# Five expert tiles from an early table, the rest of the table beside them, and scatters held until the step's denominators are summed

## The chip, the cores and the metric

The kernel runs on one core of one Trainium2 chip. The metric is device time in microseconds for one launch, taken on that core. TensorE is called PE, VectorE DVE, ScalarE ACT, GpSimd POOL and SyncE SP, as the profile does.

## The reference, cut to what matters

64 images are cut into 169 patches each (10,816 tokens of 128 features). The tokens go through a linear attention block and then through eight experts, of which each token takes its best two.

```python
concat = jnp.concatenate((x, lu, ru, ld, rd), axis=1)            # five shifted copies of each image
normed = (concat - mean) * rsqrt(var + EPS) * gamma + beta
h = conv(normed, W, stride 8).reshape(B, D, 169).transpose(0, 2, 1)     # B=64, D=128

q, k, v = split(layernorm(h) @ Wqkv.T)                           # 8 heads of 64
q_prime = exp((q * scale) @ proj.T);  k_prime = exp(k @ proj.T)
D_inv   = 1.0 / (einsum("bhnf,bhf->bhn", q_prime, k_prime.sum(axis=2)) + 1e-6)
context = einsum("bhmf,bhmd->bhfd", k_prime, v)
h = h + (einsum("bhnf,bhfd->bhnd", q_prime, context) * D_inv[..., None]) @ Wout.T + bout

topv, topi = top_k(layernorm(h) @ Wg, 2);  w = softmax(topv)
for e in range(8):                                               # y starts at zero
    y += gw[..., e] * ((silu(x @ W[e]) * (x @ V[e])) @ W2[e])    # x = layernorm(h), F = 512
h = h + y
```

## The kernel before, in words

**Token stage.** Images are taken two at a time: 32 pairs (NPAIR), in groups of four steps (k = 0 to 3) for which one patch preparation is made ahead. `step(n, k, ...)` is written once for each engine and unrolled over n = 0 to 34. In step n four pairs are in work at once: pair n is convolved and normalised (flag `a`), pair n-1 gets its keys, queries and context (`b`), pair n-2 its attention output (`c`), pair n-3 its routing to experts (`d`). Steps 32 to 34 are the drain: `a` is off, then `b`, then `c`. Each engine runs its own list in order; semaphores tie the lists.

**Inside a step, PE** does q features 0 and 1 of pair n-1, the softmax denominators of pair n-2 (line 578, 32 small products into bank 7, counted by `d8_done`), the convolution of pair n (line 585), q feature 2, then the broadcast of the inverted denominators (line 529), for which it needs DVE's chain: `dsum` (line 874, waits for `d8_done`), reciprocal (876), rounding (888, 894). Keys, the attention output (647), the context (698, 704), the residual with the gate's logits (667) and the folded output weights (711) follow. Two products (552, 553) add up how many earlier tokens chose each expert: the `ranks`, kept in bank 2, which the residual product also uses.

**DVE** finds the two best experts (`best`, `choose`) and in `place` turns ranks into row numbers (`sloti`, line 1020). The running counts per expert are in `counts`.

**POOL** takes two roots a step for the layer norms (lines 1225, 1227) and scatters: for each pair six indirect DMAs (line 1245) write 128 rows each to `sorted_rows` in DRAM, sorted by expert. In step n it issues the rows of pair n-4: three before the first layer norm's root and three after it, when `sloti` and the weights are there and `d8_done` shows the denominators of the **previous** step. In step 31 and in the drain it scatters pair n-3 as well, three, then two scatters before the second root.

**Between the stages.** After step 34 DVE makes the table of the 92 expert tiles of 256 rows (lines 1034 to 1061; row number, expert, and how many output DMAs to wait for), all on one partition. SP and ACT write pad rows behind each expert's last row (line 354). PE runs idle products (543: 2, 3 and 8 of them; 717: 39) meanwhile. Then SP waits for the table, the pads and all scatters, and loads the first tile's rows (line 1330).

**Expert stage.** Per tile PE turns the rows (two products, line 1344), makes both hidden products (24, line 1356) and the output (16, line 1368); ACT copies the expert's weights (1391) and takes the silu (1407); DVE splits weights and rows into two parts (1422, 1433), multiplies (1440) and scales the output by the gate (1446, 1448); POOL adds two times 128 rows to the output in DRAM (line 1483). A tile's scaling waits for the landing of the additions two tiles before, since they share a buffer. Additions of a tile also wait for those of the tile before, unless both belong to one expert. The unused tiles of the 92 are the first ones; they read and write pad rows.

## Time and profile before

| | us |
|---|---|
| median of 3 runs | 1214.05 (1208.42, 1214.05, 1215.71) |
| the profiled execution's own time | 1208.1 |
| its span in the trace | 1206.3 |
| granted PE clock, mean share of full speed | 0.976 |
| busy: PE, DVE, ACT, POOL | 1119.9, 878.5, 561.3, 627.1 |
| first turn of rows of the expert stage | 742.12 from the start |

The profile page gives each engine's busy time over the whole span, then the chain of work that ended last, then the costliest groups of instructions with the idle time that stood in front of them and what ended it. A busy share is a mean over two stages that have different limits, so the steps of the token stage are best read one at a time. A released wait named "remote" is one whose end the profile cannot tie to an instruction that ended just then. Ends of PE's instructions are modelled; the events of its semaphores are recorded.

### The profile page before, as it was taken

How to read it: one execution, taken by the hardware profiler on the slowest of the kernel's cores; microseconds unless marked ns; L12 is line 12 of the kernel's file. 1: busy time of each engine (PE TensorE's matmuls, PEld its weight loads, DVE VectorE, ACT ScalarE, POOL GpSimd, SP SyncE). 2: the span in 40 equal slices, each digit the busy share in tenths (PEclk: the TensorE clock that was granted, in tenths of full speed). 3: DMA queues.
4: the chain of work that ended last, by engine and by line, in shares of the span. 5: the costliest groups of instructions: out<-in, count | busy, mean ns of one | idle time of the engine just before them, and what ended most of it. 6: DMA issues, size and time to landing. Idle time of an engine off the chain costs nothing.

```text
span 1206.3 us, 30227 instructions
## 1 busy us (share of the span) xinstructions
PE 1119.9 (93%) x8672; PEld 949.0 (79%) x8673; DVE 878.5 (73%) x3310; ACT 561.3 (47%) x1307; POOL 627.1 (52%) x656
## 2 busy tenths in 40 slices
PE   4899999899899899999998779999999999999996
PEld 4577667667677676676666558999999999999995
DVE  6477777777687777776875656777777777777774
ACT  3534435436345354354333213555555555555552
POOL 0014435344444344354443544677777777777675
PEclk9899999999999899999999989999999999999999
DMA  8160201210301202110010313344344444444442
GB/s 179 39 178 26 76 24 35 71 31 29 75 31 37 62 29 68 35 33 27 28 31 22 89 49 84 48 59 54 51 54 53 58 53 55 53 54 55 56 55 29
DMA packets 76010, 65.58 MB, mean 54 GB/s; under 512 B 12339, under 2 KB 66803, under 8 KB 75927
## 3 DMA queue, kind: packets, MB, share of 16 engines
q0 software_dynamic: 32704, 24.99, 14.8%
q1 hardware_dynamic: 41990, 38.71, 12.9%
q10 hardware_dynamic: 1232, 0.85, 0.3%
q8 instruction: 42, 0.69, 0.2%
q14 instruction: 42, 0.34, 0.1%
HBM read 32.81 MB, written 31.71 MB: 53 GB/s over the span
## 4 chain that ended last, share of the span: by engine, by line
PE 67%; DVE 16%; issue 5%; another core or an unknown queue 4%; DMA 2%; POOL 2%; ACT 1%; SPq 1%; POOLq 0%; DVEq 0%; ACTq 0%
PE bank L1356 20%; PE bank L1368 13%; PE bank L647 5%; PE bank L698 4%; DVE patches L798 3%; PE bank L685 3%; PE bank L711 3%; PE bank L687 3%; PE bank L686 3%; PE bank L704 2%; DVE rparts L888 2%; PE bank L447 2%; PE bank L585 2%; DVE rden L876 2%
## 5 line engine op out<-in xcount | busy, mean ns | idle before, releaser
L1483 POOL DMA_INDIRECT out_rows<-yo,dest x184 | 327.6, 1780 | 135.6 <-issue 89.4
L1356 PE MATMUL bank<-xT_e,wv 128*128 128x256 f32 x2208 | 287.0, 285 | 0.9 <-DVE xT_e L1433 0.9
L1356 PEld LDWEIGHTS bank<-xT_e,wv 128*128 128x128 f32 x2208 | 270.1, 189 | 1.2 <-DVE xT_e L1433 1.2
L1245 POOL DMA_INDIRECT sorted_rows<-xrow_all,sloti x192 | 190.0, 990 | 62.3 <-issue 52.3
L1407 ACT ACTIVATE sil<-bank 128x256 f32<-128x256 f32 x368 | 141.1, 384 | 160.8 <-PE bank L1356 141.4
L1368 PE MATMUL bank<-w,hid 128*128 x1472 | 179.7, 275 | 2.7 <-DVE hid L1440 2.7
L1368 PEld LDWEIGHTS bank<-w,hid 128*128 128x128 f32 x1472 | 171.5, 192 | 3.2 <-issue 3.2
L1440 DVE TENSOR_TENSOR hid<-sil,bank 128x256 f32<-128x256 f32 x368 | 145.0, 417 | 25.1 <-ACT sil L1407 22.2
L1422 DVE TENSOR_TENSOR wv<-wv_all,wv 128x1024 fp32r<-128x1024 f32 x92 | 112.7, 1225 | 67.7 <-issue 36.3
L1160 ACT ACTIVATE attn<-bank 128x256 f32<-128x256 f32 x128 | 49.3, 386 | 196.2 <-PE bank L687 164.8
L1391 ACT CAST wv<-wv_all 128x1024 fp32r x92 | 96.2, 1046 | 39.0 <-issue 39.0
L1265 POOL COPY xrow_all<-xrow_all 128x384 f32<-128x384 f32 x32 | 16.1, 503 | 178.1 <-issue 159.7
L585 PE MATMUL bank<-patches,wct 128*128 128x338 f32 x320 | 101.0, 463 | 0.0
L1225 POOL TENSOR_SCALAR vare<-mv 128x3 f32<-128x3 f32 x64 | 12.4, 193 | 165.4 <-issue 117.4
L798 DVE TENSOR_TENSOR patches<-bank,gam 128x416 f32<-128x416 f32 (+3 forms) x160 | 71.6, 502 | 26.3 <-PE bank L447 25.6
L711 PE MATMUL bank<-wvo,attn 128*64 128x136 f32 x1024 | 76.4, 288 | 6.2 <-ACT attn L1155 4.0
L585 PEld LDWEIGHTS bank<-patches,wct 128*128 128x128 f32 x320 | 59.3, 193 | 28.7 <-issue 1.1
L647 PE MATMUL bank<-attn 128*128 128x169 f32 x512 | 79.5, 307 | 0.6 <-DVE attn L855 0.6
L529 PE MATMUL bank<-rparts,pick_head 104*128 104x340 f32 x128 | 47.5, 372 | 33.7 <-DVE rparts L894 32.0
L1175 ACT ACTIVATE attn<-bank 128x512 f32<-128x512 f32 x96 | 57.4, 598 | 44.8 <-PE bank L687 39.0
L647 PEld LDWEIGHTS bank<-attn 128*128 128x128 f32 x512 | 73.9, 189 | 1.7 <-DVE attn L855 0.8
L1155 ACT COPY attn<-bank 128x272 f32<-128x272 f32 x128 | 49.8, 390 | 48.4 <-PE bank L711 41.8
(191 smaller groups left out, 1936.2 us busy)
## 6 DMA issues: line engine op xcount, KB each, us to landing
xr<-sorted_rows SPq DMA_DIRECT2D x92, 130.0 KB
raw<-in_x SPq DMA_DIRECT2D x64, 84.5 KB
raw<-in_x SPq DMA_DIRECT2D x60, 78.0 KB
out_rows<-attn SPq DMA_DIRECT2D x64, 58.5 KB
sorted_rows<-xrow_all,sloti POOLq DMA_INDIRECT x192
out_rows<-yo,dest POOLq DMA_INDIRECT x184
wv_all<-in_L_ffn_W SPq DMA_DIRECT2D x8, 256.0 KB, 5.6
wv_all<-in_L_ffn_V SPq DMA_DIRECT2D x8, 256.0 KB, 5.7
```

Source lines behind the costliest of these rows:

```text
L585: t = pe.matmul(bank[1][:, 0:PT], wct[:, q], patches[:, par, q, 2 * k:2 * k + 2].rearrange("p b t -> p (b t)"), start=(q == 0), stop=(q == 4))
L647: t = pe.matmul(bank[7][:, TOK * i:TOK * i + TOK], mm[:, pc, i, j, 0:D], qf[:, pc, j, TOK * i:TOK * i + TOK], start=(j == 0), stop=(j == 3))
L711: t = pe.matmul(o_[64 * (h % 2):64 * (h % 2) + 64, col:col + D + HEADS], gT[:, i, NF * h:NF * h + NF], wvo[:, h], start=True, stop=True)
L798: t = ve.tensor_tensor(dst[:, lo:hi], src[:, i0:i0 + hi - lo, :, dy:dy + NP1], gam[:, q, lo:hi].unsqueeze(2).to_broadcast([128, hi - lo, G ...
L1245: po.indirect_dma_start(sorted_rows, bass.IndirectOffsetOnAxis(sloti[:, p, j, ch:ch + 1], 0), xrow[:, p, j, ch], None).then_inc(s(f"scatte ...
L1356: q = pe.matmul(bank[fc][:, TT * m:TT * m + TT], wv[:, w, w_, m, cols], xT[:, p, x_], start=(w_ + x_ == 0), stop=(w_ == 1))
L1368: q = pe.matmul(bank[4 + p][:, D * a:D * a + D], hid[:, p, fc, 128 * a:128 * a + 128], w2[:, bass.ds(e, 1), fc].rearrange("p e n -> p (e n ...
L1391: ac.copy(wv[:, w, 0].rearrange("p m n -> p (m n)"), wv_all[:, bass.ds(e, 1)].rearrange("p e m n -> p (e m n)")).then_inc(s("w_high"), 1)
L1407: ac.activation(sil[:, fc % 2], bank[fc][:, 0:TT], ACT.Silu).then_inc(s("silu_done"), 1)
L1422: ve.tensor_tensor(wv[:, w, 1].rearrange("p m n -> p (m n)"), wv_all[:, bass.ds(e, 1)].rearrange("p e m n -> p (e m n)"), wv[:, w, 0].rear ...
L1440: ve.tensor_tensor(hid[:, p, fc], sil[:, fc % 2], bank[fc][:, TT:2 * TT], ALU.mult).then_inc(s("h_done"), 1)
L1483: po.indirect_dma_start(out, bass.IndirectOffsetOnAxis(dest[:, p, a:a + 1], 0), yo[:, p, a], None, compute_op=ALU.add).then_inc(s(f"added{ ...
```

## The change

- `ranks` move from bank 2 to bank 5. Their products no longer wait for bank 2 and wait instead for the key exponents that last read bank 5; the next step's q feature 1 waits until the ranks are read. While `a` is on, DVE runs `place` after the attention residual, not before it.
- POOL's scatters of pair n-4 wait for the denominators of step n itself (`d8_done` one higher). The rows of pairs 28 and 29 are now scattered this way too. In steps 32 to 34 POOL waits after three of a pair's scatters until they have landed.
- After step 30 (28 pairs counted) DVE makes an early table of five tiles out of full tiles of the first experts. SP loads the rows of tiles 0 and 1 in step 32, ACT and DVE prepare weights for tiles 0 to 3 in steps 32 and 33, PE turns tile 0 in step 33 and multiplies it in step 34. All idle products before the experts but three are gone.
- After the last counts DVE alternates: tile 0, a part of the remaining table, tile 1, the rest. That table has one tile per partition, so its operations are one to 64 elements wide; PE turns it into a row in tile 3 and DVE copies it in.
- SP writes all pad rows, loads rows of tiles 2 to 4 between them, and waits for all scatters only before tile 5. POOL writes its two output pads at the start. The number of tiles stays 92; the unused ones come after tile 4.

```diff
+FIRST_TILES, NEARLY_PAIRS = 5, NPAIR - 4
...
-        ranks = bank[2][:, 0:(NCH + 1) * E]
+        ranks = bank[5][:, 0:(NCH + 1) * E]
...
+                if n == NPAIR:
+                    sp.wait_ge(s("early_ready"), 3)
+                    for q in range(2):
+                        sp.wait_ge(s(f"scattered{q}"), NEARLY_PAIRS // 2 * 96)
+                    expert_sync(sp, "early_rows", 0)
+                    expert_sync(sp, "early_rows", 1)
...
+            expert_sync(sp, "early_rows", 2)
             sp.wait_ge(s("ends_ready"), 1)
-            pad_ends(sp, range(0, E, 2))
+            pad_ends(sp, range(0, E // 2))
+            expert_sync(sp, "early_rows", 3)
+            pad_ends(sp, range(E // 2, E))
+            expert_sync(sp, "early_rows", 4)
             for q in range(2):
                 sp.wait_ge(s(f"h2_out{q}"), NPAIR // 2 * 16 * len(PLACES))
-            sp.wait_ge(s("table_ready"), 2)
-            first = [expert_sync(sp, "row_number", t) for t in range(2)]
+            sp.wait_ge(s("table_ready"), 1)
+            first = expert_sync(sp, "row_number", FIRST_TILES)
...
                 def rank():
                     pe.wait_ge(s("before_step"), NCH * (md + 1))
-                    if a:
-                        pe.wait_ge(s("ln1_x"), n + 1)
-                    else:
-                        pe.wait_ge(s("h2_copied"), n - 2)
-                        pe.wait_ge(s("logit_read"), n - 2)
+                    if b:
+                        pe.wait_ge(s("k_exp"), NCH * mb + 2)
...
-                    for j in range(2):
-                        q_feature(j)
+                    q_feature(0)
+                    at_least(pe, s("rank_read"), n - 3)
+                    q_feature(1)
...
+                if n == NPAIR + 1:
+                    expert_tensor(pe, "turn")
+                if n == NPAIR + 2:
+                    expert_tensor(pe, "first")
                 if d and not a and not b:
-                    idle_products((2, 8)[n - NPAIR - 1])
                     rank()
...
-            for _ in range(39):
-                pe.matmul(bank[0][:, 0:256], ident, cst[:, 0:256], start=True, stop=True)
-            expert_tensor(pe)
+            expert_tensor(pe, "others")
...
+                if n == NPAIR + 1:
+                    expert_vector(ve, "weights", range(1))
...
+                if n == NPAIR + 1:
+                    expert_vector(ve, "weights", range(1, 2))
+                    expert_vector(ve, "rows", 0)
-                if d:
+                if d and not a:
                     place(md, pd, 96 * half(-3))
 ...
+                if d and a:
+                    place(md, pd, 96 * half(-3))
...
+                if n == NEARLY_PAIRS + 2:
+                    early_table()          # 17 chained operations, then 3 that write the table
...
             ve.tensor_copy(ends[:], endf[:]).then_inc(s("ends_ready"), 1)
+            expert_vector(ve, 0)
+            # first part of the table: 11 operations
+            expert_vector(ve, 1)
+            # second part: 10 operations, the last two into `entry`
+            expert_vector(ve, 2)
...
+                if n == NPAIR:
+                    expert_scalar(ac, "weights", range(2))
+                if n == NPAIR + 1:
+                    expert_scalar(ac, "weights", range(2, 4))
+                    expert_scalar(ac, "rows", 0)
...
-                if a and n > 3:
-                    wait_alone(po, setup_met, (s("sloti_ready"), md), (s("w1_ready"), md), (s("d8_done"), md + 1))
+                if 3 < n < NPAIR + 2:
+                    wait_alone(po, setup_met, (s("sloti_ready"), md), (s("w1_ready"), md), (s("d8_done"), md + 2))
                     scatter(range(1), 1 - pd)
                     scatter(range(1, 2), 1 - pd, (0,))
...
-                if a and n > 3:
+                if 3 < n < NPAIR + 2:
+                    if not a:
+                        po.wait_ge(s(f"scattered{1 - pd}"), 96 * ((md - 1) // 2) + 48)
                     scatter(range(1, 2), 1 - pd, (1,))
                     scatter(range(2, NCH), 1 - pd)
-                late = n + 1 < NPAIR
-                before_root = {NPAIR: 3, NPAIR + 1: 2}.get(n, 1)
+                late = n < NPAIR + 1
...
                 if d and not late:
                     wait_alone(po, setup_met, (s("sloti_ready"), md + 1))
-                    scatter(range(before_root, NCH))
+                    scatter(range(1, 2), which=(0,))
+                    po.wait_ge(s(f"scattered{pd}"), 96 * (md // 2) + 48)
+                    scatter(range(1, 2), which=(1,))
+                    scatter(range(2, NCH))
...
+        def turn_table():
+            pe.wait_ge(s("entry_ready"), 2)
+            pe.wait_ge(s("y_scaled"), 2)
+            for at, c in enumerate((3, 0, 4)):
+                q = pe.matmul(bank[5][0:1, 128 * at:128 * at + n], entry[:, c:c + 1], ident[0:n, 0:n], ...)
...
+        if what == "first":
+            pe.wait_ge(s("early_ready"), 3)
+            pe.wait_ge(s("h2_copied"), NPAIR)
+            pe.wait_ge(s("logit_read"), NPAIR)
+            step(0, 0, 0, 0, True, False, True)
+            return
...
+        po.wait_ge(s("early_ready"), 3)
+        for t in range(FIRST_TILES):
+            add(t, t // 2, t % 2)
+        po.wait_ge(s("table_ready"), 1)
```

## Rows read from the trace of the kernel before

**Rows 1.** The page: the chain that ended last, share of the span.
```profile
PE 67%; DVE 16%; issue 5%; another core or an unknown queue 4%; DMA 2%; POOL 2%; ACT 1%; SPq 1%; POOLq 0%; DVEq 0%; ACTq 0%
```

**Rows 2.** Groups by line: busy us, mean ns | idle us before, releasers.
```profile
L1422 DVE TENSOR_TENSOR wv<-wv_all,wv 128x1024 fp32r<-128x1024 f32 x92 | 112.7, 1225 | 67.7 <-issue 36.3 <-PE bank L1356 31.4
...
L874 DVE TENSOR_SCALAR dsum<-bank 128x86 f32<-128x86 f32 x32 | 7.9, 248 | 61.5 <-remote 44.8 <-PE bank L578 16.8
...
L1016 DVE TENSOR_TENSOR pslot<-slots,pick 128x48 f32<-128x48 f32 x32 | 6.4, 201 | 0.0
```

**Rows 3.** Timeline, step 28 (k=0): start us, us, engine line [idle <-releaser].
```profile
600.25 0.25 DVE L874 TENSOR_SCALAR dsum<-bank 128x86 f32<-128x86 f32 x1 [0.72 <-PE bank L578]
...
601.89 0.96 POOL L1245 DMA_INDIRECT sorted_rows<-xrow_all,sloti  x1 [0.30 <-issue]
```

**Rows 4.** Timeline, step 30 (k=2), the same lines.
```profile
638.47 0.60 PEld L578 LDWEIGHTS bank<-attn 128*32 128x32 f32 x32 [0.22 <-issue]
...
639.02 1.06 POOL L1245 DMA_INDIRECT sorted_rows<-xrow_all,sloti  x1 [0.20 <-issue]
...
643.93 0.25 DVE L874 TENSOR_SCALAR dsum<-bank 128x86 f32<-128x86 f32 x1 [5.78 <-remote]
...
646.85 0.19 PEld L529 LDWEIGHTS bank<-rparts,pick_head 104*128 104x128 f32 x1 [4.35 <-DVE rparts L894]
```

**Rows 5.** Timeline, steps 26 and 27 (k=2, k=3), line 874 alone.
```profile
558.13 0.25 DVE L874 TENSOR_SCALAR dsum<-bank 128x86 f32<-128x86 f32 x1 [3.28 <-remote]
...
580.68 0.25 DVE L874 TENSOR_SCALAR dsum<-bank 128x86 f32<-128x86 f32 x1 [1.93 <-remote]
```

**Rows 6.** Windows, one line-874 start to the next, steps 2 and 3.
```profile
62.05:81.07 19.02, 18.52 (x143) 13.74 (x144) 13.23 (x50) 7.16 (x19) 2.09 (x4) 1.00 0.89 264
81.07:100.50 19.43, 19.33 (x150) 14.44 (x151) 16.34 (x72) 7.24 (x20) 2.96 (x8) 1.00 0.03 9
```

**Rows 7.** Windows, steps 24 to 31: us, PE, PEld, DVE, ACT, POOL busy, PEclk, DMA, GB/s.
```profile
517.45:536.11 18.66, 18.43 (x142) 13.74 (x142) 14.29 (x72) 11.17 (x30) 9.66 (x17) 1.00 0.11 33
536.11:558.13 22.02, 21.61 (x156) 15.80 (x156) 16.03 (x74) 10.75 (x23) 11.67 (x18) 1.00 0.11 35
558.13:580.68 22.55, 19.83 (x143) 14.91 (x142) 16.53 (x75) 7.25 (x20) 8.59 (x14) 0.92 0.08 26
580.68:600.25 19.57, 17.71 (x144) 13.19 (x143) 16.53 (x73) 7.25 (x20) 7.12 (x13) 1.00 0.07 22
600.25:621.16 20.91, 20.72 (x148) 14.96 (x147) 13.46 (x67) 7.24 (x20) 11.49 (x18) 1.00 0.12 37
621.16:643.93 22.77, 19.34 (x142) 13.80 (x140) 13.34 (x66) 7.25 (x20) 9.65 (x15) 1.00 0.11 32
643.93:666.25 22.32, 19.14 (x135) 14.29 (x135) 13.38 (x66) 7.25 (x20) 8.44 (x14) 0.92 0.08 23
666.25:684.66 18.41, 15.94 (x129) 11.56 (x127) 13.33 (x67) 6.76 (x19) 8.45 (x14) 1.00 0.10 29
```

**Rows 8.** Timeline of the drain and of the way to the experts.
```profile
706.72 0.68 ACT L1155 COPY attn<-bank 128x272 f32<-128x272 f32 x2 [3.63 <-remote]
...
722.53 0.16 DVE L974 TENSOR_TENSOR gap<-top 128x3 f32<-128x3 f32 x1
...
735.17 0.97 POOL L1245 DMA_INDIRECT sorted_rows<-xrow_all,sloti  x1 [0.30 <-issue]
...
742.12 0.41 PE L1344 MATMUL bank<-cst,xr 128*128 128x128 f32 x2
```

**Rows 9.** Timeline of the first expert tiles: additions and turns of rows.
```profile
754.08 2.12 POOL L1483 DMA_INDIRECT out_rows<-yo,dest  x1 [0.30 <-issue]
...
757.94 0.38 PE L1344 MATMUL bank<-cst,xr 128*128 128x128 f32 x2
758.77 2.04 POOL L1483 DMA_INDIRECT out_rows<-yo,dest  x1 [2.57 <-DMA out_rows<-yo,dest]
```

**Rows 10.** Windows, ten later expert tiles, same columns as group 7.
```profile
1003.82:1052.60 48.78, 48.78 (x423) 48.78 (x421) 37.76 (x100) 28.46 (x60) 36.09 (x21) 1.00 0.41 54
```

More of the change, by code:

```diff
@@ L1271, in step @@
                     wait_alone(po, setup_met, (s("sloti_ready"), md + 1), (s("w1_ready"), md + 1))
-                    scatter(range(before_root))
+                    scatter(range(1))
                 if c:
@@ L1281, in _, with experts @@
             steps(po, step)
-            expert_gpsimd(po)
-def experts(nc, ctx, s, met, ffw2, out, K, ident, table, wv_all, sorted_rows, bank):
+            expert_gpsimd(po, "adds")
+def experts(nc, ctx, s, met, ffw2, out, K, ident, table, entry, wv_all, sorted_rows, bank):
     def sb(name, shape, dt=F32):
@@ L1380, in step, with scalar @@
             hidden(t, p, w, 3)
-        pe.wait_ge(s("table_ready"), 2)
-        turn(0, 0, 0)
-        steps(step)(pe)
+        if what == "turn":
+            turn(0, 0, 0)
+            return
+        if what == "first":
[3 more added lines that the diff above has]
+            step(0, 0, 0, 0, True, False, True)
+            return
+        steps(step, 1)(pe)
         down(NT - 1, 1, expert_of(pe, NT - 1))
-    def scalar(ac):
+    def scalar(ac, what, which=None):
         def high_w(t, w):
@@ L1407, in step, with vector @@
                 ac.activation(sil[:, fc % 2], bank[fc][:, 0:TT], ACT.Silu).then_inc(s("silu_done"), 1)
-        ac.wait_ge(s("table_ready"), 2)
-        ac.wait_ge(s("weights_in"), 16 * 2 * E)
-        ac.wait_ge(s("conv_done"), NPAIR)
-        high_w(0, 0)
-        high_w(1, 1)
-        copy_x(0, 0, 0)
+        if what == "weights":
+            ac.wait_ge(s("early_ready"), 3)
+            ac.wait_ge(s("weights_in"), 16 * 2 * E)
+            ac.wait_ge(s("conv_done"), NPAIR)
+            for t in which:
+                high_w(t, t)
+            return
+        if what == "rows":
+            copy_x(0, 0, 0)
+            return
         steps(step)(ac)
-    def vector(ve):
+    def vector(ve, what, which=None):
         def low_w(t, w):
@@ L1449, in scale, with read_table @@
             q.then_inc(s("y_scaled"), 1)
+        def read_table():
+            n = NT - FIRST_TILES
+            ve.wait_ge(s("table_mm"), 1)
+            ve.tensor_copy(table[:, FIRST_TILES:].rearrange("o t c -> o c t"),
+                           bank[5][0:1, 0:3 * 128].rearrange("o (c t) -> o c t", c=3)[:, :, 0:n]).then_inc(s("table_ready"), 1)
+            ve.wait_ge(s("table_ready"), 1)
         def step(t, h, p, w, more, prev, more2):
-            if more:
+            if more and not (isinstance(t, int) and t < 1):
                 low_w(t + 1, (w + 1) % 4)
@@ L1463, in step, with gpsimd @@
             product(t, p, 3)
-        ve.wait_ge(s("table_ready"), 3)
-        ve.wait_ge(s("weights_in"), 16 * 2 * E)
-        low_w(0, 0)
-        meta(0, 0, 0)
-        low_x(0, 0)
-        steps(step)(ve)
+        if what == "weights":
+            ve.wait_ge(s("weights_in"), 16 * 2 * E)
+            for t in which:
+                low_w(t, t)
+            return
+        if what == "rows":
+            meta(0, 0, 0)
+            low_x(0, 0)
+            return
+        if what in (0, 1):
+            step(what, 0, what, what, True, what > 0, True)
+            return
+        steps(step, what)(ve)
         scale(NT - 1, NT // 2 - 1, 1)
-    def gpsimd(po):
+    def gpsimd(po, what):
         def add(t, h, p):
@@ L1484, in add @@
                                       compute_op=ALU.add).then_inc(s(f"added{p}"), 16)
-        pad = K("padrow").rearrange("p (a n) -> p a n", a=2)
-        for p in range(2):
-            po.dma_start(out[NTOK + 128 * p:NTOK + 128 * p + 128], pad[:, p, 0:D]).then_inc(s(f"added{p}"), 16)
-        po.wait_ge(s("table_ready"), 3)
-        add(0, 0, 0)
-        add(1, 0, 1)
-        with po.Fori(1, NT // 2) as i:
+        if what == "pads":
+            pad = K("padrow").rearrange("p (a n) -> p a n", a=2)
+            for p in range(2):
+                po.dma_start(out[NTOK + 128 * p:NTOK + 128 * p + 128], pad[:, p, 0:D]).then_inc(s(f"added{p}"), 16)
+            return
+        po.wait_ge(s("early_ready"), 3)
+        for t in range(FIRST_TILES):
+            add(t, t // 2, t % 2)
+        po.wait_ge(s("table_ready"), 1)
+        add(FIRST_TILES, FIRST_TILES // 2, FIRST_TILES % 2)
+        with po.Fori((FIRST_TILES + 1) // 2, NT // 2) as i:
             add(2 * i, i, 0)
```

158 lines of the change are left out of this document (108 added, 50 removed).

## The prediction

> **What bounds the kernel now.** I began with the page: PE fills 67% of the chain that ended last, but 4% of that chain is "another core or an unknown queue", in a kernel that uses one core [rows 1]. Next came the groups by line. The largest such wait stands in front of DVE's line 874, which waits for PE's denominators: 61.5 us idle in 32 steps, of which 44.8 end "remote" and 16.8 with PE [rows 2]. The timeline by step gives 15 waits of the first kind and 17 of the second, so this is no average: two kinds of step exist, and each has to be read.
>
> In step 28 line 874 starts at 600.25 after 0.72 us of waiting, and POOL's scatters come after it [rows 3]. In step 30 PE issues the same product at 638.47, a scatter starts at 639.02, and line 874 starts only at 643.93, after 5.78 us; PE then stands 4.35 us before the broadcast that needs the inverted denominators [rows 4]. In steps 26 and 27 the waits are 3.28 and 1.93 [rows 5]. I went through all 32: the 15 late ones (every k=2 and k=3 from step 6 on, and steps 29 to 31) are exactly those of steps 6 to 31 in which the first scatter starts before line 874. Steps 2 and 3 are k=2 and k=3 too, but nothing is scattered yet (POOL busy 2.09 and 2.96 us); they last 19.02 and 19.43 us, where steps 26 and 27 last 22.55 and 19.57 [rows 6, 7]. Where a late step leaves PE standing long, the granted clock reads 0.92 of full speed, thus part of it at 1.2 GHz [rows 7].
>
> Later tiles of the expert stage have no room: ten tiles take 48.78 us with PE busy for all of it, DVE for 37.76, POOL for 36.09 [rows 10]. Nothing of the change works there. Its two places are the scatters' order and the way from step 32 to the fifth tile.
>
> **The scatters' order.** They now wait for the product of their own step, so all steps become like step 28, where POOL's first triple lies beside PE's convolution. Extra waiting removed: 44.8 - 15 x 0.72 = 34.0 us [rows 2, 3]. I take it in full, since in step 30 PE idles 4.35 of the 5.06 extra [rows 4]; the other end is 4.35/5.06 of it, 29. Clock: a reading of 0.92 over some 22.4 us is 1.8 us at the full rate. Six k=2 steps (6, 10, ... 26) and step 30 have it, and two of the k=3 steps read the same: 9 x 1.8 = 16 us [rows 7]; the other end is half, 8. Check by periods: a group is 18.66 + (22.02 - 2.56) + (22.55 - 1.21 - 1.8) + 19.57 = 77.2 us; steps 4 to 27 lie between 100.50 and 600.25, which is 499.75, so six such groups save 36.5. The last four windows sum to 84.41; less 13.5 - 2.2 = 11.3 of waits (44.8 less six times 5.21, over three steps) and 1.8 of clock they give 71.3, 13.1 less. Both ways give 50. The root behind the triple loses nothing: in k=0 and k=1 the order is already this one, at 1.00 of the clock [rows 7].
>
> **Ranks and `place`.** The rank products (two) keep their place on PE and read bank 5, last used by key exponents that are over by then; q feature 1 of the next step waits for a read that DVE has made one normalisation earlier. `place` behind the residual lets PE's residual product start sooner and makes `sloti` later by less than 1 us; only the next step's scatters use it, a step later. Nothing, between -1 and +1 us over all steps. If this cover went, PE would stand before q feature 1.
>
> **The early table** sits on DVE between step 30 and line 874 of step 31. 20 operations at 0.20 us, as that of line 1016 [rows 2], are 4.0 us; 0.7 of them cover waiting that is there anyway, so PE's broadcast comes 3.3 late. With some clock lost: +4, between +2 and +6. Step 31 so stays about as long as it was.
>
> **The drain.** A stall like those above also hits ACT at 706.72: 3.63 us "remote", while POOL issues six scatters in a row [rows 8]. Threes with a wait between end this, but DVE's weight split for tile 0, 1.2 us [rows 2], now stands before step 33's denominators, behind a routing that ends about when they do, so I count 1.8 of the 3.6. The first expert products wait for the logits' copy, before the row at 722.53; with weights and residual in the way they start about 721 instead of 743.4 (after the turn at 742.12) [rows 8]. That is 22 us, but most is given back. DVE reaches tile 0's four products only behind step 34's routing, at about 726, and then has table parts of some 2.8 and 2.2 us between tiles 0, 1 and 2 (21 operations again at 0.2 to 0.25). At 37.76/10 busy us a tile and its gaps, 4.3, it stands at tile 3 at about 743.
>
> POOL is later still. From about 718 it has the last two pairs: twelve scatters at 0.96 + 0.30 us [rows 3], a root and the copies (2.7) and two waits for landings, 1.5 us each by my estimate, below the 2.57 that an addition waits [rows 9] as the queues are emptier. The last ends at about 739.5, where it now ends at 736.1 (735.17 + 0.97) [rows 8]. Only then comes tile 0's addition, and tile 2's scaling waits for its landing: 3.6 us of issue and 2.6 of landing [rows 9], 745.9. So tile 3's second half starts at about 745.7, the time of the turn that now stands at 757.94 [rows 9]: 12 us sooner. Unused tiles now come after the fifth: one more addition that must wait for the one before, +1. Tile 5's rows need the last landing and a load, together 742.12 - 736.14 = 6.0 us now [rows 8], thus 745.5, and are wanted at 750: covered; without the cover each us is paid once. What is late next is thus POOL's first addition. Sum: -11 net of the drain stall, between -16 (DVE's chain alone decides) and -4 (each of four waits for landings 3 us, half of those 6.0, and not 1.5).
>
> Idle products: behind step 33 PE now has gaps until tile 3. In the token stage such gaps cost 1.8 us each [rows 7]; one is in the range. The Trainium skill's page "TensorE: Matmul & The Clock Gate", part 1, says that an idle PE falls back to half rate, which speaks against removing them; by it one or two tiles would be slow, 2 to 4 us, and the trace agrees as far as it has such rows. POOL's output pads move to the start, where POOL is idle: 0. The six early loads lie on SP behind the output weights, where it is idle; the 8 pad writes on one queue instead of two are needed only at tile 5: 0.
>
> **The sum.** -50 + 4 - 11 = -57 on the profiled execution's 1208.1 (span 1206.3), so 1151. The median of the runs, 1214.05, is 0.5% above it: 1157. I say 1158. Own range: -29 - 8 + 6 - 4 + 1 = -34 to -50 + 2 - 16 - 1 = -65, on 1214 thus 1149 to 1180; runs that come out as the lowest of before (1208.4) put the low end at 1143.
>
> **Rivals.** *The scatters are not the cause* (0.12). For it: the page "SBUF — State Buffer" of the Trainium skill, in "Who interferes with whom", states that DMAs do not contend with compute engines and that PE waits on no one; by that a scatter in flight can't hold up a completion of PE, and moving it buys nothing. As a mechanism of this kernel: the late waits would come with k=2 and k=3 themselves. Then -50 falls away, the early table's cost remains half hidden in a wait, and the transition brings 11: 1214 - 11 + 2 = 1205. Against it: steps 2 and 3 [rows 6], and step 29, a k=1 step, whose 22.77 follows a late wait of its own [rows 7].
>
> *The transition pays nothing* (0.13): the last triples' landings and cold PE eat it. Token stage alone: 1214 - 46 = 1168 to 1170. For it: POOL's list grows by 3 us and gates the additions.
>
> *The stall moves along* (0.05): what is held is any completion of PE while a triple is in flight, now the convolution's and q feature 2's, in all 29 steps instead of 15. Then DVE's residual 906 is late by what line 874 was: 28 x 2.3 (34.0/15) = 64 instead of 34, +30 with no clock regained, +4 for the early table, -11: 1237, slower. It decides once half of the steps show it. Against it: in step 28 and in every k=0 and k=1 step the triple already flies there, and those windows have PE busy 18.43 of 18.66 [rows 7].
>
> *Partly moved* (0.10): a third to a half of the stalls stay, at 1180 to 1195.
>
> **How the numbers follow.** The forecast has 0.60, at 1158. No change within 1% (about what a measurement of this kernel can tell) is 1202 to 1226: the first rival, and little of the partial one. Faster: 0.60 + 0.13 + 0.09 = 0.82; same 0.11 + 0.01 = 0.12; slower 0.05 + 0.01 = 0.06. One hundredth of the partial case counts as no change and one of the first as slower. The range for 8 in 10 takes in the forecast's own, the second rival and most of the partial one, and leaves out the first and the third: 1143 to 1190.
>
> **What would show it.** Right: line 874 after no "remote" wait and about 0.7 us in every step but 31, where it starts some 3 to 4 us behind the early table; 0.97 or more of the clock over steps 4 to 30; groups of 77 us; step 32's line 874 near 640, not 684.66; the turn of tile 4's rows 60 to 62 us behind it, now 757.94 - 684.66 = 73.3; DVE's line 1446 waiting for a landing at tile 2. Wrong: late events of PE at lines 585 or 687 instead, POOL's root of the first norm later than 6 us behind line 874, or the expert stage's period above 4.88.

## The result

| | before | after |
|---|---|---|
| median, us | 1214.88 of 4 runs | 1158.24 of 4 runs |
| profiled execution, us | 1208.1 | 1159.75 |
| its span, us | 1206.3 | 1158.0 |
| granted PE clock, share | 0.976 | 0.983 |
| line 874 (902 after) of step 2 to step 32, us | 622.6 | 577.9 |
| from there to the end, us | 521.7 | 514.7 |

The ratio of the times is 0.9535 (95% interval 0.9486 to 0.9585): faster, 1158.24 where 1158 was forecast. One of the four runs of after took 1364.31 us at a granted clock of 0.751; the ratio leaves it out, but the median counts it, and without it the median is 1156.74.

Lines have moved: 874 is 902, the denominators' product 578 is 605, the scatter 1245 is 1323, the broadcast 529 is 558, the turn of rows 1344 is 1428, the addition 1483 is 1612, the scaling 1446 is 1559. Shares of the chain that ended last, after; these answer to [rows 1]:

```profile
PE 79%; DVE 9%; SPq 4%; issue 3%; DMA 3%; ACT 1%; POOL 0%; POOLq 0%; DVEq 0%; ACTq 0%
```

The unknown releaser's 4% is gone. In the groups by line, after [rows 2]:

```profile
L558 PE MATMUL bank<-rparts,pick_head 104*128 104x340 f32 x128 | 42.9, 337 | 6.5 <-DVE rparts L922 4.7 <-DVE attn L881 1.8
...
L1559 DVE CAST dest<-meta_ 128x2 uint32<-128x2 f32 x92 | 16.1, 175 | 11.2 <-PE bank L1457 5.7 <-DMA out_rows<-yo,dest 4.2 <-remote 1.3
...
L902 DVE TENSOR_SCALAR dsum<-bank 128x86 f32<-128x86 f32 x32 | 7.9, 247 | 20.5 <-PE bank L605 20.3
```

Line 902 now waits 20.5 us in 32 steps where it waited 61.5, and never "remote". The timeline of step 30, after, which answers to [rows 4]:

```profile
601.49 0.80 PE L605 MATMUL bank<-attn 128*32 128x86 f32 x32
...
602.43 0.25 DVE L902 TENSOR_SCALAR dsum<-bank 128x86 f32<-128x86 f32 x1 [1.28 <-PE bank L605]
...
603.15 1.06 POOL L1323 DMA_INDIRECT sorted_rows<-xrow_all,sloti  x1 [1.36 <-PE bank L605]
```

The product takes 0.94 us from PE's issue to DVE's reading, not 5.46, and the scatter follows. Windows of steps 26 to 32, after, in the columns of [rows 7]:

```profile
527.59:547.00 19.41, 18.80 (x146) 14.04 (x145) 16.79 (x76) 7.25 (x20) 9.14 (x15) 1.00 0.10 31
547.00:565.61 18.61, 18.40 (x148) 13.79 (x147) 15.60 (x72) 7.25 (x20) 8.83 (x14) 1.00 0.09 27
565.61:584.03 18.42, 18.21 (x138) 13.31 (x138) 13.49 (x67) 7.26 (x20) 9.19 (x15) 1.00 0.11 32
584.03:602.43 18.40, 18.19 (x138) 13.30 (x138) 13.50 (x66) 7.25 (x20) 9.09 (x14) 1.00 0.11 32
602.43:623.46 21.03, 20.82 (x148) 15.10 (x147) 16.81 (x87) 7.25 (x20) 10.68 (x16) 1.00 0.12 37
623.46:643.30 19.84, 17.38 (x129) 12.80 (x129) 13.47 (x68) 7.25 (x20) 7.44 (x13) 0.91 0.07 22
643.30:665.40 22.10, 13.88 (x115) 9.53 (x114) 13.49 (x68) 7.81 (x17) 10.12 (x15) 1.00 0.48 129
```

The rows are those of steps 26 to 32. Steps 26 and 29 are 3.1 and 4.4 us shorter, and step 26 reads 1.00 of the clock instead of 0.92. The rows of steps 30 and 31, at 21.03 and 19.84 us, are those around the early table; step 31's alone still reads 0.91.

Step 2's line 902 comes at 65.4, 3.4 us later than before. The experiments below show it anywhere from 61.6 to 68.1, the same kernel included (65.3 and 61.6), so that start is spread between executions and not the change. I therefore compare the stretches in the table: -44.7 and -7.0.

These two differences have a spread of their own. The kernel before, traced once more (experiment 12), has 624.3 and 518.5 where the table has 622.6 and 521.7. Against that trace the changed kernel gains 46.4 and 3.8.

### The profile page after: what moved, and what is told of

It reads as the page before. It is cut to its first block, busy times and chain, and to the rows that moved or that the text cites. A ratio compares the mean times of both kernels' runs of the same rounds, so it can differ in the third digit from the quotient of the medians.

```text
span 1158.0 us, 29957 instructions
## 1 busy us (share of the span) xinstructions
PE 1088.3 (94%) x8580; PEld 924.0 (80%) x8581; DVE 882.1 (76%) x3333; ACT 561.7 (49%) x1307; POOL 613.2 (53%) x656
## 4 chain that ended last, share of the span: by engine, by line
PE 79%; DVE 9%; SPq 4%; issue 3%; DMA 3%; ACT 1%; POOL 0%; POOLq 0%; DVEq 0%; ACTq 0%
PE bank L1440 21%; PE bank L1457 13%; PE bank L677 6%; PE bank L612 5%; PE bank L726 5%; PE bank L739 4%; PE bank L713 4%; PE bank L715 3%; PE bank L714 3%; PE bank L732 3%; DVE patches L824 2%; PE bank L605 2%; PE bank L476 2%; PE bank L1428 2%; DMA out_rows<-yo,dest 2%
## 5 line engine op out<-in xcount | busy, mean ns | idle before, releaser
L1612 POOL DMA_INDIRECT out_rows<-yo,dest x184 | 312.4, 1698 | 140.4 <-issue 107.0
L1440 PE MATMUL bank<-xT_e,wv 128*128 128x256 f32 x2208 | 291.9, 288 | 5.4 <-DVE xT_e L1546 3.5
L1440 PEld LDWEIGHTS bank<-xT_e,wv 128*128 128x128 f32 x2208 | 273.9, 191 | 6.1 <-DVE xT_e L1546 4.0
L739 PEld LDWEIGHTS bank<-wvo,attn 128*64 128x64 f32 x1024 | 56.7, 136 | 14.6 <-ACT attn L1229 6.9
L726 PE MATMUL bank<-attn,xtok 128*128 128x512 f32 x128 | 67.9, 612 | 0.0
```

The source lines that it names most:

```text
L726: pe.matmul(bank[(6, 1)[i]][:, :], xtok[:, p, i], kf[:, i], start=True, stop=False)
L739: t = pe.matmul(o_[64 * (h % 2):64 * (h % 2) + 64, col:col + D + HEADS], gT[:, i, NF * h:NF * h + NF], wvo[:, h], start=True, stop=True)
L1440: q = pe.matmul(bank[fc][:, TT * m:TT * m + TT], wv[:, w, w_, m, cols], xT[:, p, x_], start=(w_ + x_ == 0), stop=(w_ == 1))
L1612: po.indirect_dma_start(out, bass.IndirectOffsetOnAxis(dest[:, p, a:a + 1], 0), yo[:, p, a], None, compute_op=ALU.add).then_inc(s(f"added{ ...
```

## The experiments

The experiments ran on four chips. On three of them (5, 3 and 2) the kernel before took 1209 to 1215 us, as in the result above; on chip 3 that is a single run. On one, chip 4, it took 1161.16 (19 runs). That was no part of any theory, and it is read below. In the table, "step 2 to 32" is the time from the line of the denominators (874 in before) in step 2 to that in step 32, and "behind" is the time from there to the end, both in the profiled execution. A group of four is four steps, measured between such lines.

| kernel | us | ratio to before, same chip | step 2 to 32 | behind | chip |
|---|---|---|---|---|---|
| 1 before, scatters' wait changed | 1162.75 | 0.9623 (0.9600 to 0.9647) | 575.0 | 517.9 | 5 |
| 2 after, wait put back | 1203.30 | 0.9966 (0.9934 to 0.9999) | 627.0 | 512.5 | 5 |
| 3 after, rows 0 and 1 first | 1158.10 | one run | 577.3 | 510.8 | 5 |
| 4 as 1, three direct DMAs early | 1164.01 | one run | 579.2 | 519.6 | 5 |
| 5 as 1 | 1159.38 | 0.9985 (0.9967 to 1.0003) | 574.9 | 519.9 | 4 |
| 6 after | 1154.71 | 0.9942 (0.9921 to 0.9962) | 577.6 | 514.3 | 4 |
| 7 after, four moves | 1149.55 | 0.9898 (0.9872 to 0.9924) | 574.4 | 511.6 | 4 |
| 8 as 1, seven POOL copies early | 1212.71 | one run | 627.8 | 520.0 | 4 |
| 9 one scatter early | 1172.78 | one run | 590.3 | 518.1 | 3 |
| 10 as 8 | 1217.65 | one run | 628.8 | 523.7 | 3 |
| 11 as 7 | 1151.71 | 0.9509 (0.9481 to 0.9538) | 574.4 | 511.5 | 2 |
| 12 before | 1212.34 | one run | 624.3 | 518.5 | 2 |

**1. The order alone.**

```diff
-  ... (s("w1_ready"), md), (s("d8_done"), md + 1))
+  ... (s("w1_ready"), md), (s("d8_done"), md + 2))
```

> The kernel before with one number changed: POOL's first triple of scatters waits for the denominators' product of its own step (d8_done md + 2) and not of the step before. Theory (scatters in flight hold PE's completions back): all 32 waits of line 874 end with PE after about 0.7 us, groups of four steps take 77.2 us instead of 82.8 to 84.3, and the token stage gives 45 to 50 us: 1160 to 1169. Rival 1 (the scatters are not the cause, the gain is that of the rest of the change): 1205 to 1215, groups still 83 to 84. Rival 2 (the stall at line 874 goes but the whole loop is bounded by something else that the changed place of the ranks and of `place` relieves): waits gone, groups 79 to 81, 1180 to 1195.

The group of line 874, and the last four steps by windows:

```profile
L874 DVE TENSOR_SCALAR dsum<-bank 128x86 f32<-128x86 f32 x32 | 7.9, 248 | 24.6 <-PE bank L578 24.3
```

```profile
566.70:585.12 18.42, 18.22 (x138) 13.31 (x138) 13.47 (x66) 7.26 (x20) 9.18 (x15) 1.00 0.11 32
585.12:603.53 18.41, 18.21 (x138) 13.30 (x138) 13.50 (x66) 7.25 (x20) 9.09 (x14) 1.00 0.11 32
603.53:621.97 18.44, 18.22 (x138) 13.31 (x138) 13.52 (x67) 7.26 (x20) 9.09 (x14) 1.00 0.11 33
621.97:640.53 18.56, 18.19 (x137) 13.20 (x136) 13.48 (x66) 6.77 (x19) 10.93 (x16) 1.00 0.13 39
```

One number in a wait is worth 46 us (0.0377 x 1209), the theory's 45 to 50. The six groups from step 4 to step 28 take 77.0 to 77.4. The waits are not all the 0.7 us I had said: those where k is 3 are 0.03 to 0.05 and those of steps 29 to 31 are 1.3. Both rivals fall: the waits end with PE, and nothing else of the change was needed.

**2. The change without the order.** The diff above, the other way, in the changed kernel.

> The changed kernel with the scatters' wait put back (d8_done md + 1); early table, rest of the table, places of ranks and `place`, threes and early tiles in the drain as changed. Theory: the stalls come back, groups of 83 to 84 us, +40 to +48 on the changed kernel's 1156, thus 1196 to 1204; the rest of the change keeps its 7 to 10 us. Rival (order and the rest only work together): either 1156 to 1165 (the order was not what brought it), or 1210 and above (the drain and early table alone cost what they bring).

```profile
L902 DVE TENSOR_SCALAR dsum<-bank 128x86 f32<-128x86 f32 x32 | 7.9, 247 | 58.0 <-remote 45.0 <-PE bank L605 12.9
```

The waits are back, with groups of 82.4 to 84.0 up to step 28; steps 28 to 31, which hold the early table too, take 90.6. The rest alone brings 0.3% here. By stretches the part up to step 32 is 4.4 us longer than in the profile of before and what lies behind it 9.2 shorter (2.7 and 6.1 against the trace of experiment 12). The number fits the theory's upper end; the rest's 4 us are less than the 7 to 10 said.

**3. Rows 0 and 1 first.** SP issues the loads of tiles 0 and 1 behind its wait for the last convolution, ahead of the output weights and of step 32's outputs.

```diff
                 if n == NPAIR:
                     sp.wait_ge(s("conv_done"), NPAIR)
+                    sp.wait_ge(s("early_ready"), 3)
+                    ... scattered{q}; early_rows 0 and 1
                     for e in range(E):
                         expert_sync(sp, "down_weights", e)
```

> The changed kernel, with SP issuing the loads of tile 0's and 1's rows right behind its wait for the last convolution, before the output weights and the outputs of step 32's pair. Theory (PE's 6.30 us wait for tile 0's rows in step 33, at 668.05, is SP's list and not the scatters' landings): the wait falls to under 1 us, step 33's broadcast comes 2 to 3 us sooner (DVE's inverted denominators are ready at 668.3, the broadcast now starts at 671.2), and the run ends 2 to 3 us sooner: span 1155 to 1156 instead of 1158.0. Rival (DVE's chain of routing, weight splits and denominators is what step 33 goes by, or POOL's scatters behind it): wait gone, the turn of tile 4's rows stays 61.5 to 62.5 us behind step 32's line 902, span 1157.5 to 1158.5.

It was aimed at these lines of the changed kernel, timeline of step 33:

```profile
665.40 0.24 DVE L902 TENSOR_SCALAR dsum<-bank 128x86 f32<-128x86 f32 x1
...
665.85 1.58 SPq L1412 DMA_DIRECT2D xr<-sorted_rows  x2
...
668.05 0.69 PE L1428 MATMUL bank<-cst,xr 128*128 128x128 f32 x2 [6.30 <-DMA xr<-sorted_rows]
...
671.16 1.13 PE L558 MATMUL bank<-rparts,pick_head 104*128 104x340 f32 x2
```

With the loads first the turn of rows has no wait and step 33's broadcast waits for DVE instead (3.39 us for the inverted denominators). Measured from step 32's line 902, the broadcast comes only 0.9 us sooner, where I had said 2 to 3. The whole stretch behind that line is 3.9 us shorter than in the changed kernel's profile, and tile 4's turn comes 60.2 us behind it where it was 62.4. The span, 1156.3, is at the theory's edge only because this execution started 2.7 us later.

**4. Direct DMAs in the scatters' old place.** Base: experiment 1.

```diff
+  wait_alone(po, setup_met, ..., (s("d8_done"), md + 1))
+  for i in range(3):
+      po.dma_start(spare_rows[bass.ds(128 * (3 * (n - 4) + i), 128)], cst[:, 0:RW])...
   wait_alone(po, setup_met, (s("d8_done"), md + 2))
```

> The kernel before with its scatters behind the denominators' product as in the changed kernel, and at the old early moment (behind the d8 product of the step before) three direct DMAs issued by POOL, 128 rows of 130 floats each from the constants to a DRAM area of their own, in 28 steps. It does more work than the kernel before; the output is the same. Theory A (what holds PE's completions is a DMA of POOL's queue in flight, of any form): late waits of line 874 come back at the same places, 3 to 5 us where k is 2 or 3, span near 1200. Theory B (it is the indirect form, its descriptors or its scattered writes): line 874 waits about 0.7 everywhere, groups at 77 to 78, span near 1160. Theory C (it is POOL's own work of issuing): a direct DMA takes POOL 0.59 us in the trace of before, so the wait is 0.5 to 1.5 longer and no 'remote' in it.

Timeline of step 26 (k=2), and the group:

```profile
527.98 0.80 PE L580 MATMUL bank<-attn 128*32 128x86 f32 x32
...
528.33 1.77 POOL L1255 DMA_DIRECT2D spare_rows<-cst  x3
...
528.86 0.25 DVE L876 TENSOR_SCALAR dsum<-bank 128x86 f32<-128x86 f32 x1 [0.69 <-PE bank L580]
```

```profile
L876 DVE TENSOR_SCALAR dsum<-bank 128x86 f32<-128x86 f32 x32 | 7.9, 248 | 24.1 <-PE bank L580 23.9
```

POOL issues the DMAs from 0.35 to 2.12 us behind the product's issue, as early as the scatters in [rows 4], and the product is read 0.88 us after its issue. Theory B: POOL's queue with direct DMAs holds nothing, on a chip where three scatters cost 46 us. The extra DMAs are not free: the groups take 77.5 to 78.1.

**5, 6, 7. The rest of the change, and four moves.**

> The kernel of the first experiment once more (the kernel before, only the scatters' wait changed), timed beside the changed kernel itself on one chip, to weigh the rest of the change. By the profiles the rest costs 3.8 us in steps 28 to 31 (the early table) and brings 3.2 behind step 32's line 902, so it is worth nothing: ratio to the kernel before 0.955 to 0.962, and within 3 us of the changed kernel. Rival (the forecast's own sum, -7 for the rest, and the earlier ratios 0.9535 and 0.9623): 5 to 10 us behind the changed kernel.

> The changed kernel as it is, beside the one with the scatters' wait alone. By the profiles: within 3 us of it. By the forecast's sum: 5 to 10 us faster.

The four moves: those of experiment 3; rows 3 and 4 ahead of the second half of the pads; `expert_vector(ve, "weights", range(1))` behind `rden_ready` instead of before line 902; and in step 30

```diff
+                if n == NEARLY_PAIRS + 2:
+                    early_table()
                 if c:
                     ve.wait_ge(s("h2_copied"), mc + 1)
```

> The changed kernel with four steps moved: SP's loads of rows 0 and 1 ahead of the output weights and step 32's outputs; rows 3 and 4 both ahead of the second half of the pads; DVE's weight split for tile 0 behind step 33's inverted denominators instead of before line 902; the early table in step 30 before DVE's wait for the copied outputs, where DVE stands idle 1.9 us. Theory (these are where the forecast's -11 in the transition went, and part of the +4): 4 for the rows (one look gave 514.7 - 510.8 behind step 32's line 902), 2 for the split (line 902 of step 33 starts at 667.2 and not 669.5 in that look), 1.9 for the pads, 1.9 for the table, of which overlaps leave 6 to 9 us: 1148 to 1152 where the changed kernel has 1157. Rival (POOL's last scatters and first additions are what the fifth tile waits for, as the prediction had it): 1153 to 1156, the turn of tile 5's rows not before 67 us behind step 32's line 902.

All on chip 4. The changed kernel is 4.7 us faster than the order alone (ratios 0.9942 and 0.9985), between the two expectations. By stretches the rest costs 2.7 up to step 32 and brings 5.7 behind it. The first figure has two parts: steps 28 to 31 take 77.7 instead of 73.7, +4.0, and the six groups before them take 461.4 instead of 462.7, about 0.2 less each, -1.3. I put that down to the new places of the ranks and `place`, since no other part of the change reaches there; no run moves them alone.

The four moves bring 5.2 more, to 1149.55. That is inside the 1148 to 1152 I had said, but I had counted from 1157 and expected 6 to 9. Steps 28 to 31 give 3.2 of it, where I had expected 1.9 for the early table. Behind step 32's line they give 2.7, no more than the rows' loads alone had given on chip 5 (3.9), so the moves of the pads and of the weight split are not shown to add anything. Tile 5's turn comes 65.3 us behind step 32's line, 68.5 in experiment 6. In step 33 DVE's line for the denominators comes right behind the routing, the weight split behind the inverted ones, and the broadcast starts 3.1 us after the line (660.89), 5.8 in the changed kernel:

```profile
657.21 0.57 DVE L1063 TENSOR_TENSOR before<-before,both 128x8 fp32r<-128x8 f32 x3
...
657.82 0.25 DVE L899 TENSOR_SCALAR dsum<-bank 128x86 f32<-128x86 f32 x1
...
661.00 1.22 DVE L1534 TENSOR_TENSOR wv<-wv_all,wv 128x1024 fp32r<-128x1024 f32 x1 [0.16 <-issue]
```

**8 and 10. POOL busy, no DMA.** Base: experiment 1, as in 4, with seven copies of 128x384 on POOL in place of the DMAs.

> The kernel before with its scatters behind the denominators' product as in the changed kernel, and at the old early moment seven copies of 128x384 on POOL (0.50 us each in the trace of before, 3.5 us together, as long as three scatters), in 28 steps, no DMA. Extra work; the output is the same. Theory A (POOL being busy holds PE's completions or DVE back): late waits of line 874 come back where k is 2 or 3, 2 to 4 us each, span 1185 to 1200. Theory B (it is the indirect DMA in flight): waits of about 0.7 us everywhere, span 1158 to 1164; DVE's own instructions beside the copies may be longer.

> The kernel with seven POOL copies at the early moment once more. On a chip where the kernel before takes 1206 to 1216: theory A (POOL's being busy is what holds PE's completions) gives line 874 waits above 3 us where k is 2 or 3 and a time above 1225; theory B (only an indirect scatter in flight does) gives waits of about 0.7 us and the time of the last look, 1208 to 1216, made of DVE's copies beside POOL's: L889 1.86 us where it was 0.83. On a chip where the kernel before takes 1157 to 1167 it repeats 1212.7.

Groups of the second run (chip 3, where before takes 1214.58):

```profile
L1257 POOL COPY scratch<-scratch 128x384 f32<-128x384 f32 x196 | 101.2, 517 | 10.4
...
L895 DVE TENSOR_TENSOR rparts<-rden,rparts 32x86 fp32r<-32x86 f32 (+1 forms) x128 | 52.7, 412 | 2.4
...
L889 DVE CAST rparts<-rden 32x86 fp32r<-32x86 f32 (+1 forms) x128 | 42.8, 334 | 2.4
...
L875 DVE TENSOR_SCALAR dsum<-bank 128x86 f32<-128x86 f32 x32 | 7.9, 248 | 25.1 <-PE bank L579 24.8
```

The copies were meant to keep POOL busy across the product. In step 26 of the run on chip 3 they run from 0.34 to 4.32 us behind the product's issue, and line 875 reads it after 0.87. So a busy POOL is not the cause (chip 4 could not have shown it). My figure for the first run's time (1158 to 1164) missed by 49 us all the same, and the second run, 1217.65, lies just above the 1208 to 1216 said. Two things in these traces are longer: DVE's casts and subtractions beside the POOL copies take 0.33 to 0.36 and 0.39 to 0.41 us on average instead of 0.24, and POOL's triple and the root behind it come 2.9 us later (in the first run scatters 3.66 us behind line 875, not 0.78; DVE then waits 1.21 for the root in step 28). Groups last 84.7, 7.6 more than without. How much of the 7.6 each of the two brings is not shown.

**9. One scatter early, two behind the product.**

```diff
   wait_alone(po, setup_met, ..., (s("d8_done"), md + 1))
-  scatter(range(1), 1 - pd)
+  scatter(range(1), 1 - pd, (0,))
+  wait_alone(po, setup_met, (s("d8_done"), md + 2))
+  scatter(range(1), 1 - pd, (1,))
   scatter(range(1, 2), 1 - pd, (0,))
```

> The kernel before with one of the triple's three scatters at the old early moment (behind the d8 product of the step before) and two behind the product of the step itself; nothing else changed. The runs of the kernel before beside it tell which kind of chip this is: 1206 to 1216 as in the first two comparisons, or 1157 to 1167 as in the last one. On the first kind, theory A (the hold lasts as long as any indirect scatter is in flight): late waits where k is 2 or 3, but 2.6 us shorter than with three (two issues of 0.96 + 0.30 less), thus some 2.0 to 2.5 us in k=2 of the later groups and about none in k=3; span 1170 to 1185. Theory B (it takes a second scatter behind the first to hold PE): no late wait, span 1158 to 1164. On the second kind no late wait under either, 1157 to 1164.

Timeline of step 26, and below it the same step with three early (experiment 2):

```profile
533.87 0.80 PE L578 MATMUL bank<-attn 128*32 128x86 f32 x32
...
534.44 1.06 POOL L1245 DMA_INDIRECT sorted_rows<-xrow_all,sloti  x1 [0.20 <-issue]
...
535.87 0.25 DVE L874 TENSOR_SCALAR dsum<-bank 128x86 f32<-128x86 f32 x1 [1.81 <-PE bank L578]
```

```profile
556.40 0.60 PEld L605 LDWEIGHTS bank<-attn 128*32 128x32 f32 x32 [0.22 <-issue]
...
556.98 1.06 POOL L1323 DMA_INDIRECT sorted_rows<-xrow_all,sloti  x1 [0.20 <-issue]
...
558.34 0.96 POOL L1323 DMA_INDIRECT sorted_rows<-xrow_all,sloti  x1 [0.30 <-issue]
559.61 0.96 POOL L1323 DMA_INDIRECT sorted_rows<-xrow_all,sloti  x1 [0.30 <-issue]
...
559.87 0.25 DVE L902 TENSOR_SCALAR dsum<-bank 128x86 f32<-128x86 f32 x1 [3.28 <-remote]
```

From the product's issue to its reading: 2.00 us with one scatter, 3.47 with three, 0.9 with none or with direct DMAs. Groups of four take 79.1, 82.4 to 84.0 and 77.1. So one indirect scatter is enough, and more of them hold longer (one on chip 3, three on chip 5): theory A, at 1172.8, though its waits are 1.8 us where k is 2, below the 2.0 to 2.5 said, and 1.24 where k is 3, where it had none. It is not a hold until the last one lands, since line 902 starts while the third is still being issued. With one scatter, line 874 starts 0.37 us after POOL is done issuing it. Whether the issuing or the transfer holds is therefore not separated by these runs.

What is late is the completion and not DVE. The traces record the update of the semaphore that line 874 waits for: 0.85 us behind the product's issue in step 26 of experiment 1, 1.97 with one scatter, 3.44 with three, and 5.36 in step 30 of the kernel before. DVE starts 0.02 to 0.10 us after it each time, and in experiment 9 POOL, which waits for the same number, starts its next scatter 0.75 us after DVE does, as in experiment 1 (0.78). A DVE kept off by something of its own, such as a port that POOL holds, falls as a rival. The wait of 1.81 us above is labelled with PE and is held all the same, so the label "remote" is no measure of the hold.

**11 and 12. The four moves against the usual kind of chip, and the kernel before again.**

> The changed kernel with the four moves once more. On a chip where the kernel before takes 1206 to 1216: ratio to it 0.9535 (the changed kernel's) x 0.9898/0.9942 = 0.949, between 0.945 and 0.954, 1146 to 1154. On a chip where the kernel before takes 1157 to 1167: 0.990 again. If the four moves' gain is worth nothing where PE's completions can be held (their loads and writes fall beside the drain's scatters), the first ratio stays at 0.953 or above.

> The kernel before, unchanged, for its trace on this chip. If it takes 1206 to 1216, the waits of line 874 are those known: 55 to 65 us in all, groups of 82 to 85 us. If it takes 1157 to 1167: line 874 waits 22 to 26 us in all, none of it late, the first scatter still before line 874 where k is 2 or 3, groups of 77.0 to 77.5: the same order of the program, and no completion held.

```profile
L874 DVE TENSOR_SCALAR dsum<-bank 128x86 f32<-128x86 f32 x32 | 7.9, 248 | 61.2 <-remote 45.0 <-PE bank L578 16.2
```

The kernel before has on chip 2 the waits of [rows 2] within 0.3 us. The four moves stand at 1151.71, and on both kinds of chip theirs is the lowest time I measured. The intervals of 0.9509 and 0.9535 overlap; that the moves are worth 5 us is shown on chip 4, where both ran side by side.

## Why the prediction was right

- **The scatters' order, -50.** Right in cause, 4 us too large. Experiment 1 gives -46 in time and 575.0 - 622.6 = -47.6 in the stretch. The six groups gave 37.1, forecast 36.5. The last four steps gave 84.4 - 73.8 = 10.6, forecast 13.1: I subtracted waits until 71.3 was left, 17.8 a step, but such a step cannot be shorter than PE's own 18.2 us of work, which the windows of experiment 1 show in all four. The row of step 28 in [rows 7], with PE busy 20.72 of 20.91 though step 29's late wait lies in it, could have warned me that PE fills part of such a wait with work of its own. The clock term held: all windows of steps 4 to 30 read 1.00 in the changed kernel, where nine of them read 0.92.
- **Ranks and `place`, 0 (-1 to +1).** Just outside: they brought about 1.3 us (0.2 in each of six groups), if nothing else reached there.
- **The early table, +4.** +3.8 between the changed kernel and experiment 1, +4.0 between 6 and 5. The table runs from 619.60 to 623.5, 20 operations in 3.9 us, and line 902 starts at 623.46 behind it. It covers 1.3 us of waiting that is there without it, not 0.7, so line 902 is 2.6 us late; the window's 0.91 of the clock is 1.8 us more. The two sum to 4.4, a little over what was measured.
- **The transition, -11.** Tile 4's turn stands 62.4 us behind step 32's line, forecast 60 to 62 and 73.3 before: -10.8. At the end only -7.0 is left. Part of both is the one profile of before: its second trace has tile 4's turn at 71.1 and leaves -3.8, and side by side on chip 4 the turn moves from 71.2 to 62.9 and the stretch behind the line shrinks by 5.7. The term was thus too large by 4 to 7 us. The step that failed is "the six early loads lie on SP behind the output weights, where it is idle; the 8 pad writes are needed only at tile 5: 0". SP works its list in order. Rows 0 and 1 come behind the outputs that wait for step 32's copies (the 6.30 us above), and tile 4's rows behind pads. The timeline around tile 4, after:

```profile
701.74 0.71 SPq L373 DMA_DIRECT2D sorted_rows<-cst  x1
...
703.31 8.59 SPq L1412 DMA_DIRECT2D xr<-sorted_rows  x3
...
705.75 0.44 PE L1428 MATMUL bank<-cst,xr 128*128 128x128 f32 x2 [1.86 <-DMA xr<-sorted_rows]
...
706.73 3.62 PE L1457 MATMUL bank<-w,hid 128*128 x16
...
710.39 0.17 DVE L1559 CAST dest<-meta_ 128x2 uint32<-128x2 f32 x1 [2.54 <-PE bank L1457]
...
713.06 0.38 PE L1428 MATMUL bank<-cst,xr 128*128 128x128 f32 x2
```

  The tile after the gap takes 7.3 us instead of 4.9. Additions to unlike tiles take 0.8: three later tiles of 5.3, 5.8 and 6.4 us, 2.8 over the usual 4.88 together, where before had one of 6.9, 2.0 over. That is the +1 I had said, but the one slow tile of before is 5.4 to 8.6 us in the other traces with the same expert stage. The last 0.6 or so is that 76 later tiles take 371.4 us, not 370.7.
- **"What is late next is POOL's first addition."** Wrong. The last scatter and the first addition came within 1.5 us of the forecast (56.1 and 56.4 behind step 32's line), but tile 2's scaling, the line at 710.39, waited for PE's products and not for a landing.
- **The idle products, 2 to 4 us at risk.** About 2, as the price of a PE that had stood; no run puts the idle products back, and the gap itself came from the late rows of tile 4. The window of tile 4 reads 0.77 of the clock, after one in which PE was busy for 7.08 of 9.75 us:

```profile
696.00:705.75 9.75, 7.08 (x55) 6.43 (x55) 7.30 (x27) 3.90 (x9) 6.92 (x6) 1.00 0.49 114
705.75:713.06 7.31, 7.30 (x49) 6.92 (x49) 3.75 (x11) 2.56 (x5) 3.44 (x3) 0.77 0.33 48
```

  In experiment 6, without that gap, tile 4 takes 5.62 us at 1.00:

```profile
702.86:708.48 5.62, 5.62 (x50) 5.30 (x49) 4.52 (x11) 2.83 (x7) 4.71 (x4) 1.00 0.50 58
```

  The Trainium skill's page "TensorE: Matmul & The Clock Gate", part 1, has an idle PE fall back to half rate. The trace agrees, at 1.7 us for one tile.
- **The rivals.** "The scatters are not the cause" falls with experiments 1 and 2, on the chip of the prediction's kind. On chip 4 it would have been right: there the order alone brings 0.15% (ratio 0.9967 to 1.0003), and the order-changed kernel has the same stretch up to step 32 on both kinds of chip (575.0 on chip 5, 574.9 on chip 4), so with the order changed nothing of the hold is left in that stretch. The page "SBUF — State Buffer" of the Trainium skill, in "Who interferes with whom", has DMAs not contend with compute engines and PE wait on no one; chip 4 and the direct DMAs of experiment 4 agree, the 2.00 and 3.47 us of experiments 9 and 2 do not fit what I drew from it, and the measurement decides. (The section speaks of SBUF's ports; no run shows that the hold is there.) "The stall moves along" and "partly moved" fall with those equal stretches and with the windows, where PE is busy for 18.2 of 18.4 us in step 28 and step 29; of other groups only line 1559 waits "remote", for 1.3 us. "The transition pays nothing" falls with -3.8 to -7.0.
- **The sum.** By the profiles of before and after the stretches give -44.7 - 7.0 = -51.7 against -57, and the later start takes 3.4 back: the profiled execution fell from 1208.1 to 1159.75, where the sum said 1151. That is 8.7 us off. That 1158.24 meets 1158 so closely is luck: the order and the transition brought less than said, and the medians made up for it. I had added 7 us to the figure of the profiled execution, and the median of after lies 1.5 below its own. What the prediction had right is the cause and the size of the main term.

**What stays open.** What an indirect scatter does to PE's completions, in its issuing or in its transfer, since direct DMAs of the same queue and compute on POOL do nothing. Why one chip of four shows none of it: I have the time of the kernel before there, not its trace. And whether the hold needs the profiler. On chip 4 the list of DMA issues gives a time to landing for the scatters (experiment 5, here); on the others, before and after included, the column is empty for them:

```profile
sorted_rows<-xrow_all,sloti POOLq DMA_INDIRECT x192, 2.4
```

The traces of chip 4 have 17,600 to 17,800 recorded semaphore updates, all others 13,100 to 13,700, experiments 1, 3 and 4 included, in which nothing is held up to step 32. So records are lost on the chips that can hold completions, whether or not a run does; I can't say which follows from which. The Trainium skill's page "NOTIFIC — Programmer's Manual", section "When the ring fills", says that a full queue of records can be set to drop new ones (the default), to overwrite the oldest or to stall the producer. The last would be one way for a recorder to hold a completion; no run here shows it.

## What to carry to other kernels

When a wait ends "remote", or is longer in some steps than in others, list it step by step beside what was in flight, and look for the steps where the same instruction does not wait; here that gave the cause and its size before anything was built. Move the transfer behind the completion that others wait for, rather than making the waiting engine faster. A load "behind idle SP" is free only if nothing on that queue's list ahead of it waits, and a gain that hangs on held completions has to be measured on more than one chip.

## What the runs showed that I had not expected

- The hold: 1.1 us of extra time to read a product with one indirect scatter of POOL beside it, 2.5 with three in a k=2 step (4.5 in step 30), none with three direct DMAs.
- It belongs to the chip: 1209, 1215 and 1212 us against 1161 for one and the same kernel. The expert stage, full of indirect additions, shows nothing of it: 76 tiles take 370.7 us in the kernel before and 371.1 on chip 4 with the order changed.
- POOL copies of 128x384 beside DVE's casts and subtractions of 32x84 and 32x86 stretch those from 0.24 to 0.33 and 0.41 us on average (experiment 10).
